# Keys two blocks ahead in a merged attention stage, magnitude pieces on VectorE, and semaphores cleared one stage later

## The chip, the cores and the metric

The kernel runs on one core of one Trainium2 chip. The metric is the device time of one execution in microseconds; lower is better. The time before is the median of three runs.

## The reference

A gated two-layer block on 2048 tokens of width 512 (x and a context of the same size). Layer 0 is a cross attention with 16 heads of 128 and a routed expert FFN; layer 1 is an attention in which the 16 heads of one token attend to each other, and an FFN with weights rounded to -1, 0 and 1. The part that this case is about:

```python
x = x + jnp.tanh(g_ffn[0]) * _L0_ffn_ref(_layernorm(x), ...)          # top 2 of 8 experts + shared
x = x + jnp.tanh(g_xattn[1]) * _L1_xattn_ref(_layernorm(x), ctx, ctx, ...)
x = x + jnp.tanh(g_ffn[1]) * _L1_ffn_ref(_layernorm(x), w1, b1, w2, b2)

def _L1_xattn_ref(q, k, v, Wq, bq, Wk, bk, Wv, bv, Wo, bo):
    Q = (q @ Wq.T + bq).reshape(bs, sl, H, HD)      # H = 16, HD = 32
    K = (k @ Wk.T + bk).reshape(bs, sl, H, HD)
    V = (v @ Wv.T + bv).reshape(bs, sl, H, HD)
    score = jnp.einsum('bshd,bsgd->bshg', Q, K)     # heads against heads, per token
    weight = jax.nn.softmax(score, axis=-1)
    attn = jnp.einsum('bshg,bsgd->bshd', weight, V).reshape(bs, sl, nf)
    return attn @ Wo.T + bo
# _bit_quant(w): scale = mean(|w|); ternary = clip(round(w / scale), -1, 1)
```

## The kernel before

The program is four stages, one after the other, each with its own streams for SyncE (all DMA issues of the stage but gathers), GpSimd, ScalarE, TensorE and VectorE: `l0_attention` (prefix a_), `l0_experts` (b_), `l1_attention` (p_, the merged stage) and `l1_output_ffn` (f_). The helper `stage` (L2607) runs one, ends it with a barrier of all engines, and then has GpSimd clear every semaphore of the stage, one instruction each, before GpSimd enters the next stage.

**The merged stage** does three things over four blocks of 512 tokens. It adds the experts' rows to x (two gathers by GpSimd, L1806, and `tile_stats` on VectorE, four 128-token tiles a block) and normalises each tile (`tile_normalise`). It projects keys, values and queries. And it does the attention of heads against heads. The operand splits (`w_high`, `c_high`, `h_high` on ScalarE, `..._low` on VectorE or GpSimd) give each fp32 operand a high and a low part, so a projection of one 128x512 piece is 12 matmuls.

The work of the first two kinds is a list `ITEMS`, in the order in which TensorE does it: ("k", b, j), ("v", b, j), ("q", b, j) are projections of piece j of block b, and ("h", b, j) is the transpose of the normalised tile j, which the queries need. Two PSUM banks take the items in turn, so item i waits until item i-2 was taken out. Each k, v or q piece goes through one of four slots of `outs` to DRAM (`store`), and a block's four pieces are then read back in the attention's layout (`load_k`, `load_v`, `load_q`). For the queries ScalarE then makes one more copy, `move_queries` (L1912). `ROUND` counts how often a slot has been used.

**The loop** goes over 32 pairs p, eight a block (b = p // 8, w = p % 8). Pair p does, on TensorE: `scores(p)` for two units, an item, `turn` of the two units of the pair before, a second item, and `weigh` for the pair before that. VectorE masks each unit's scores (L2150), finds the maxima (L2154), and takes the reciprocals (L2158); ScalarE does eight exponentials (L1924), takes k and q items (L1888) or the high part of h items (L1895), and copies the turned units out (L1930); GpSimd normalises (L1829). The first FIRST = 24 items run ahead of the loop, the other 40 two to a pair, so pairs 0 to 19 hold items and pairs 20 to 31 (`lean`) hold none. In a lean pair VectorE takes the reciprocal of the second unit after the mask and maxima of the next pair's first.

Beside the pairs from p = 12 on, 32 pieces of the FFN's weights are summed by magnitude for the last stage: one a pair on ScalarE, and from p = 20 one more on VectorE.

Instruction order on each engine is written out by hand. SyncE's order decides when a load or store is even tried: whatever stands behind a wait there waits too.

## Time and profile before

| | us |
|---|---|
| median of 3 runs (2204.09 to 2206.22) | 2206.16 |
| the profiled execution | 2200.77 |
| its span, first to last instruction | 2199.0 |
| merged stage: ScalarE's first instruction | 1481.47 |
| merged stage: first scores (pair 0) | 1581.19 |
| merged stage: scores of pairs 8, 16 | 1642.10, 1709.22 |
| merged stage: turns after the last pair | 1831.76 |
| last stage: first matmul of the output projection | 1849.20 |

TensorE is busy for 1969.6 us of the span (90%), GpSimd 1094.9, VectorE 1017.7, ScalarE 826.7. Times in the rows are microseconds from the span's start. A row of the timeline has the start, the time from the first start to the last end, engine, line, operation and tiles, and in brackets how long the engine stood idle ahead of it and who ended that.

### The profile page before, as it was taken

To read this page: it belongs to the slowest core of one execution; us is meant where nothing else is said; L and a number is where in the kernel's file an instruction comes from. 1 tells how busy PE (TensorE), PEld (TensorE's weight loads), DVE (VectorE), ACT (ScalarE), POOL (GpSimd) and SP (SyncE) were. 2 spreads that over 40 slices of the span, in tenths; PEclk is the share of its full clock that TensorE was granted. 3 is DMA by queue.
4 is the path that set the end of the run, shared out by engine and by line. 5 is a ranking of instruction groups with operands and counts; after the bars stand their busy time and mean duration, and the time that the engine had idled before them with its cause. 6 is when DMAs were issued, how large, how long until landed. Compare 5 with 4: busy or idle time off the path is not lost. (4 is left out here: it accounts for less than half of the span.)

```text
span 2199.0 us, 30241 instructions
## 1 busy us (share of the span) xinstructions
PE 1969.6 (90%) x10428; PEld 1649.3 (75%) x10428; DVE 1017.7 (46%) x1561; ACT 826.7 (38%) x1578; POOL 1094.9 (50%) x805
## 2 busy tenths in 40 slices
PE   6999999999999999689996999985799874789998
PEld 5888788878887888478884899983677653568886
DVE  3556654755476547623331333335466343583111
ACT  3336332633363336231211222223377763233332
POOL 6755576557655774441147646606254222533332
PEclk9999999999999999879998999997899966899999
DMA  4232323133313331362326655427676635222000
GB/s 155 82 105 68 116 96 106 53 108 116 107 48 112 101 124 30 118 214 82 139 95 204 197 164 161 131 75 210 175 187 153 169 113 184 81 68 67 19 19 19
DMA packets 173869, 251.29 MB, mean 114 GB/s; under 512 B 45040, under 2 KB 69616, under 8 KB 173744
## 3 DMA queue, kind: packets, MB, share of 16 engines
q1 hardware_dynamic: 158656, 205.23, 30.0%
q0 software_dynamic: 9472, 34.09, 4.9%
q10 hardware_dynamic: 5616, 10.23, 1.2%
q8 instruction: 88, 1.44, 0.3%
q14 instruction: 37, 0.30, 0.0%
HBM read 182.92 MB, written 66.58 MB: 113 GB/s over the span
## 5 line engine op out<-in xcount | busy, mean ns | idle before, releaser
L238 POOL TENSOR_TENSOR a_w_hl<-a_w_raw,a_w_hl 128x2048 fp32r<-128x2048 f32 x65 | 299.8, 4613 | 164.6 <-ACT a_w_hl L300 164.4
L413 PE MATMUL a_proj<-a_c_hl,a_w_hl 128*128 128x512 f32 x768 | 183.2, 399 | 21.4 <-DVE a_w_hl L530 19.6
L300 ACT ACTIVATE a_w_hl<-a_w_raw 128x2048 fp32r<-128x2048 f32 x66 | 126.2, 1912 | 164.6 <-PE a_proj L413 106.7
L413 PEld LDWEIGHTS a_proj<-a_c_hl,a_w_hl 128*128 128x128 f32 x768 | 146.2, 192 | 53.8 <-issue 19.6
L487 PE MATMUL a_proj<-a_w_hl,a_a_hl 128*128 128x512 f32 x768 | 179.5, 392 | 4.0 <-DVE a_a_hl L586 4.0
L413 PE MATMUL a_proj<-a_w_hl,a_c_hl 128*128 128x512 f32 x768 | 181.3, 392 | 0.0
L413 PE MATMUL a_proj<-a_a_hl,a_w_hl 128*128 128x512 f32 x768 | 176.4, 390 | 0.0
L319 ACT ACTIVATE a_sq<-a_proj,a_vecs 128x512 f32<-128x512 f32 x128 | 87.9, 689 | 228.6 <-PE a_proj L413 149.1
L487 PEld LDWEIGHTS a_proj<-a_w_hl,a_a_hl 128*128 128x128 f32 x768 | 142.7, 188 | 34.3 <-POOL a_w_hl L238 5.5
L413 PEld LDWEIGHTS a_proj<-a_a_hl,a_w_hl 128*128 128x128 f32 x768 | 143.6, 188 | 29.7
L262 POOL TENSOR_TENSOR a_ssum<-a_ssum,a_sq 128x512 f32<-128x512 f32 x112 | 145.6, 1300 | 36.9 <-ACT a_sq L319 33.2
L413 PEld LDWEIGHTS a_proj<-a_w_hl,a_c_hl 128*128 128x128 f32 x768 | 142.4, 188 | 28.7
L1252 PE MATMUL b_gate_up<-b_wts,b_xt_hl 128*128 x936 | 159.4, 326 | 4.2 <-DVE b_xt_hl L1451 4.2
L1252 PEld LDWEIGHTS b_gate_up<-b_wts,b_xt_hl 128*128 128x128 f32 x936 | 154.5, 190 | 8.2 <-issue 5.0
L2398 POOL TENSOR_TENSOR f_a_hl<-f_act_sb,f_a_hl 128x512 fp32r<-128x512 f32 x64 | 86.0, 1345 | 149.0 <-ACT f_a_hl L2430 148.9
L1160 PE MATMUL b_gate_up<-b_wts 128*128 128x512 f32 (+1 forms) x576 | 142.0, 407 | 3.0 <-POOL b_wts L937 2.5
L586 DVE SCALAR_TENSOR_TENSOR a_a_hl<-a_qT,a_vecs,a_a_hl 128x512 fp32r<-128x512 f32 x64 | 105.1, 1672 | 83.4 <-ACT a_a_hl L333 83.4
L1160 PEld LDWEIGHTS b_gate_up<-b_wts 128*128 128x128 f32 (+1 forms) x576 | 106.8, 186 | 34.3 <-POOL b_wts L937 2.6
L2490 PE MATMUL f_totals<-f_ternary,f_a_hl 128*128 128x512 f32 x512 | 122.5, 396 | 0.0
L2476 PE MATMUL f_hidden<-f_h_hl,f_ternary 128*128 x512 | 121.0, 394 | 0.0
L1829 POOL TENSOR_TENSOR p_probs<-p_probs,p_rden 128x512 f32<-128x512 f32 x64 | 68.0, 1068 | 99.6 <-DVE p_rden L2158 99.1
L1924 ACT ACTIVATE p_probs<-p_probs,p_mx 128x128 f32<-128x128 f32 x256 | 99.1, 390 | 47.5 <-DVE p_mx L2154 47.4
(245 smaller groups left out, 3682.5 us busy)
## 6 DMA issues: line engine op xcount, KB each, us to landing
a_w_raw<-in_a_ki_w SPq DMA_DIRECT2D x18, 1024.0 KB, 5.2
a_w_raw<-in_a_vi_w SPq DMA_DIRECT2D x16, 1024.0 KB, 5.1
a_w_raw<-in_a_q_w SPq DMA_DIRECT2D x16, 1024.0 KB, 5.1
a_w_raw<-in_a_o_w SPq DMA_DIRECT2D x16, 1024.0 KB, 5.4
b_gu_raw<-in_b_gate_up POOLq DMA_DIRECT2D x32, 352.0 KB, 3.7
l_sorted_rows<-b_zeros SPq DMA_DIRECT2D x39, 256.0 KB, 3.3
b_hs<-l_sorted_rows SPq DMA_DIRECT2D x39, 256.0 KB, 3.2
l_expert_out<-b_yg ACTq DMA_DIRECT2D x39, 256.0 KB, 3.5
```

The source lines that it names most:

```text
L238: pool.tensor_tensor(w_hl[:, s, 1], w_raw[:, s], f32(w_hl[:, s, 0]), ALU.subtract)\
L262: pool.tensor_tensor(ssum[:], first, sq[:, n % 2, :], ALU.add).then_inc(sq_added, 1)
L300: act.activation(w_hl[:, i % 2, 0], w_raw[:, i % 2], ACT.Copy).then_inc(w_high, 1)
L319: act.activation(sq[:, n % 2, :], proj[:, j, :], ACT.Square, bias=bias)\
L413: mm = pe.matmul(proj[:, j, :], left, right, start=(k == 0 and n == 0), stop=(k == KC - 1 and n == 2))
L487: mm = pe.matmul(proj[:, j, :], a_hl[:, ap, k, j * P:(j + 1) * P], w_hl[:, i % 2, wp, k], start=(n == 0 and m == 0), stop=(n == 4 * G - 1 ...
L586: dve.scalar_tensor_tensor(a_hl[:, 1, n % 4, :], qT[:, n, :], v_b[:, n:n + 1], f32(a_hl[:, 0, n % 4, :]), ALU.add, ALU.subtract).then_inc( ...
L1160: mm = pe.matmul(gu_ps[0:w, n, part, :], gu_hl[:, s, wp, k, cols], h_hl[:, hslot, ap, k, :], start=(k == 0 and m == 0), stop=(k == KC - 1 ...
L1252: mm = pe.matmul(gu_ps[:, i % 2, half, 0:F], x_part(i, xp)[:, own], part(r, P, at, F), start=(k == 0 and xp == 0 and start == HI), stop=(k ...
L1924: e = act.activation(probs[:, r, y, :], probs[:, r, y, :], ACT.Exp, bias=mx[:, r, y:y + 1], accum_out=den[:, r, y:y + 1])
L2476: mm = pe.matmul(h_ps[:, m % 2, :], w_t[:, 2 * g, k, f * P:(f + 1) * P], h_hl[:, ap, k, bass.ds(BLK * t, BLK)], start=(k == 0 and ap == 0) ...
L2490: mm = pe.matmul(y_ps[:, j, :], a_hl[:, ap, f, j * P:(j + 1) * P], w_t[:, 2 * g + 1, f, :], start=(m == 0 and ap == 0), stop=(m == NG * FC ...
```

## The change

Three things change, all in the merged stage but for the last.

1. `ITEMS` is ordered anew. Ahead of the loop stand k0, v0, h0, q0 and k1 (20 items; before k0, v0, h0, q0, h1, q1). In the loop each block b has v(b+1), h(b+1), q(b+1) and k(b+2), in this order, so the keys are two blocks ahead. Pairs 0 to 21 hold items, 22 to 31 are lean. All that serves the items moves with them: the tiles' stats from w = 0..3 to w = 4..7, the context's splits from w = 4..7 to w = 2..5, `move_queries` from w = 3 to w = 7, and SyncE's stores and loads. Ahead of the loop the low parts of the query weights go from GpSimd to VectorE, between the tiles' stats; the stats of block 1 come after all four h items of block 0; GpSimd splits one piece of context after each gather.
2. The magnitude pieces: pairs 16 to 21 one on VectorE, pairs 22 to 27 two on VectorE and one on ScalarE, pairs 28 to 31 two on VectorE (before 20 on ScalarE and 12 on VectorE, now 6 and 26).
3. The semaphores of a stage are cleared by GpSimd at the end of its stream for the next stage, ahead of that stage's barrier; those of the last stage after its barrier, as before.

In the diff stand, one after the other: the list, the pieces, GpSimd ahead of the loop and in it, ScalarE the same, VectorE ahead of the loop, and `stage`.

```diff
-    ITEMS = [(kind, b, j) for kind, b in (("k", 0), ("v", 0), ("h", 0), ("q", 0), ("h", 1), ("q", 1)) for j in range(4)]
+    ITEMS = four("k", 0) + four("v", 0) + four("h", 0) + four("q", 0) + four("k", 1)
     FIRST = len(ITEMS)
     for n in range(1, NBLK):
-        ITEMS += [("k", n, j) for j in range(4)]
+        ITEMS += four("v", n) + four("h", n) + four("q", n)
         if n + 1 < NBLK:
-            ITEMS += [("v", n, 0), ("h", n + 1, 0), ("v", n, 1), ("h", n + 1, 1), ("h", n + 1, 2), ("h", n + 1, 3),
-                      ("v", n, 2), ("v", n, 3)]
-            ITEMS += [("q", n + 1, j) for j in range(4)]
-        else:
-            ITEMS += [("v", n, j) for j in range(4)]
+            ITEMS += four("k", n + 1)
...
-        for p in range(12, NP * NBLK):
-            PIECES += [(p, "act")] + ([(p, "dve")] if p >= 20 else [])
+        for p in range(16, NP * NBLK):
+            PIECES += [(p, "dve")] * (1 if p < 22 else 2) + [(p, "act")] * (22 <= p < 28)
...
             for n in range(TPB):
                 power(n)
                 gather(n + 2)
-            for k in range(KC):
-                w_low("q", k)
             for n in range(TPB, 2 * TPB):
                 power(n)
                 gather(n + 2)
-                if n == TPB + 1:
-                    for k in range(KC):
-                        c_low(1, k)
+                c_low(1, n - TPB)
...
-                if b + 2 < NBLK and w >= NP - KC:
-                    c_low(b + 2, w - NP + KC)
+                if b + 2 < NBLK and 2 <= w < 2 + KC:
+                    c_low(b + 2, w - 2)
...
-            for j in range(TPB):
-                h_high_part(1, j)
             for j in range(4):
-                take("q", 1, j)
-                if j == 2:
+                take("k", 1, j)
+                if j == 1:
                     move_queries(0)
...
-                    if b + 1 < NBLK and w == 3:
+                    if b + 1 < NBLK and w == 7:
                         move_queries(b + 1)
...
             for j in range(TPB):
-                tile_stats(TPB + j)
                 h_low_part(0, j)
-                tile_normalise(TPB + j)
-            for j in range(TPB):
-                h_low_part(1, j)
+            tile_stats(TPB)
+            for n in range(TPB + 1, 2 * TPB):
+                tile_stats(n)
+                tile_normalise(n - 1)
+            tile_normalise(2 * TPB - 1)
...
         run(nc, new_sem, *args)
+        for s in used:
+            nc.gpsimd.sem_clear(s)
         nc.all_engine_barrier()
-        for s in own:
-            nc.gpsimd.sem_clear(s)
+        used[:] = own
```

**SyncE at the head of the merged stage.** The names: l_kT, l_vT are the stored keys and values, p_k the keys' read back (`load_k`), carry<-in_ctxT the context's load, x<-p_xr the store of x2, p_xr<-x_shared the load of x. Before:

```order
L1682 DMA l_kT<-p_outs 128x512 x4
L1661 DMA carry<-in_ctxT 128x512 x4
L1671 DMA x<-p_xr 128x512 x4
L1703 DMA p_k<-l_kT 32x16x128 x4
L1680 DMA l_vT<-p_outs 128x16x32
L1667 DMA p_xr<-x_shared 128x512
```

and now:

```order
L1681 DMA l_kT<-p_outs 128x512
L1660 DMA carry<-in_ctxT 128x512
L1702 DMA p_k<-l_kT 32x16x128 x4
L1670 DMA x<-p_xr 128x512 x4
L1679 DMA l_vT<-p_outs 128x16x32
L1666 DMA p_xr<-x_shared 128x512
```

(the first two are the last of four such turns: keys and context alternate). The keys' read moved ahead of the four x2 stores, and each context load stands right behind a key store.

**TensorE in the loop.** p_scores are a pair's scores, p_turned its turns, p_out its weighing; p_proj is an item (from p_w_hl,p_c_hl values, from p_ident,p_hn an h item). Pair 2 before:

```order
L2043 MATMUL p_scores<-p_k,carry 128x128 x8
L2028 MATMUL p_proj<-p_w_hl,p_c_hl 128x512 x12
L2052 MATMUL p_turned<-p_ident,p_probs 128x128 x8
L2008 MATMUL p_proj<-p_ident,p_hn 128x128 x4
L2065 MATMUL p_out<-p_probs,p_v 32x128 x8
```

and now:

```order
L2033 MATMUL p_scores<-p_k,carry 128x128 x8
L1998 MATMUL p_proj<-p_ident,p_hn 128x128 x4
L2042 MATMUL p_turned<-p_ident,p_probs 128x128 x8
L1998 MATMUL p_proj<-p_ident,p_hn 128x128 x4
L2055 MATMUL p_out<-p_probs,p_v 32x128 x8
```

Before, pairs 2 and 3 each held a value and an h item, and pair 4 two h items; now pairs 2 and 3 hold two h items each, and the queries come right behind them.

**GpSimd at the start of the merged stage.** ISA x84 are the clears of the experts' semaphores, x58 those of the first stage's. Before:

```order
L2618 ISA x84
L1799 UNCONDITIONAL_BRANCH
L1832 MEMSET p_ones 128x128
L1833 MEMSET p_mhalf 128x1
L1834 IOTA p_diff 128x8
```

and now:

```order
L2612 ISA x58
L1795 UNCONDITIONAL_BRANCH
L1828 MEMSET p_ones 128x128
L1829 MEMSET p_mhalf 128x1
L1830 IOTA p_diff 128x8
```

The 58 stand ahead of the barrier that ends the experts' stage, the 84 were behind it; they now stand behind the merged stage's last normalisation.

## Rows read from the trace of the kernel before

**Rows 1.** The windows view of the head: PE, PEld, DVE, ACT, POOL busy, clock, DMA.

```profile
1520.00:1530.00 10.00, 0.00 (x0) 0.00 (x0) 1.74 (x3) 0.00 (x0) 4.46 (x4) 0.56 1.01 209
```

**Rows 2.** Timeline from the end of the first stage to the start of the second.

```profile
921.76 1.77 SPq L858 DMA_DIRECT2D carry<-x  x4
...
925.83 0.20 POOL L913 MEMSET b_ones<- 128x128 f32 x1 [7.47 <-issue]
...
926.79 0.69 DVE L1296 BATCH_NORM_STATS2 b_stats<-carry 128x6 f32<-128x512 f32 x1 [7.89 <-POOL b_tile_no L918]
```

**Rows 3.** Timeline at the start of the merged stage.

```profile
1481.47 0.63 ACT L1876 ACTIVATE p_w_hl<-carry 128x512 fp32r<-128x512 f32 x1 [7.20 <-PEq L2616]
...
1487.16 0.20 POOL L1832 MEMSET p_ones<- 128x128 f32 x1 [60.93 <-issue]
...
1490.04 4.48 PE L2028 MATMUL p_proj<-p_c_hl,p_w_hl 128*128 128x512 f32 x9 [12.13 <-DVE p_c_hl L2094]
```

**Rows 4.** Timeline at the start of the last stage.

```profile
1847.91 2.91 DVE L2519 TENSOR_TENSOR f_a_hl<-f_act_sb,f_a_hl 128x512 fp32r<-128x512 f32 x2 [5.28 <-ACT f_a_hl L2414]
```

**Rows 5.** Timeline of the merged stage's head, ahead of its first scores.

```profile
1508.91 0.75 DVE L2102 SCALAR_TENSOR_TENSOR p_xr<-p_routed,weight,p_xr 128x512 f32<-128x512 f32 x1 [1.40 <-DMA p_routed<-l_expert_out,place]
...
1519.69 5.93 SPq L1667 DMA_DIRECT2D p_xr<-x_shared  x1
...
1528.19 0.75 DVE L2102 SCALAR_TENSOR_TENSOR p_xr<-p_routed,weight,p_xr 128x512 f32<-128x512 f32 x1 [9.85 <-DMA p_xr<-x_shared]
...
1531.69 0.99 POOL L1806 DMA_INDIRECT p_routed<-l_expert_out,place  x1 [0.18 <-issue]
...
1538.22 6.82 POOL L1812 TENSOR_TENSOR p_c_hl<-carry,p_c_hl 128x512 fp32r<-128x512 f32 x4 [0.43 <-ACT p_c_hl L1872]
...
1539.18 1.09 DVE L2102 SCALAR_TENSOR_TENSOR p_xr<-p_routed,weight,p_xr 128x512 f32<-128x512 f32 x1 [3.18 <-DMA p_routed<-l_expert_out,place]
...
1549.53 10.78 PE L2028 MATMUL p_proj<-p_a_hl,p_w_hl 128*128 128x512 f32 x34 [13.03 <-DVE p_a_hl L2126]
```

**Rows 6.** Timeline of TensorE in the loop over the 32 pairs.

```profile
1581.19 1.16 PE L2043 MATMUL p_scores<-p_k,carry 32*128 32x128 f32 x16
...
1582.29 5.76 PE L2028 MATMUL p_proj<-p_c_hl,p_w_hl 128*128 128x512 f32 x24
...
1595.62 1.16 PE L2043 MATMUL p_scores<-p_k,carry 32*128 32x128 f32 x16
...
1642.10 1.16 PE L2043 MATMUL p_scores<-p_k,carry 32*128 32x128 f32 x16
...
1739.12 1.16 PE L2043 MATMUL p_scores<-p_k,carry 32*128 32x128 f32 x16
...
1747.82 1.16 PE L2043 MATMUL p_scores<-p_k,carry 32*128 32x128 f32 x16
...
1815.20 1.11 PE L2052 MATMUL p_turned<-p_ident,p_probs 128*128 128x128 f32 x4 [2.13 <-POOL p_probs L1829]
...
1822.04 1.11 PE L2052 MATMUL p_turned<-p_ident,p_probs 128*128 128x128 f32 x4 [2.14 <-POOL p_probs L1829]
...
1831.76 1.14 PE L2052 MATMUL p_turned<-p_ident,p_probs 128*128 128x128 f32 x8
```

**Rows 7.** Groups by line, 1400 to 2199: busy us, mean ns, idle before.

```profile
L1924 ACT ACTIVATE p_probs<-p_probs,p_mx 128x128 f32<-128x128 f32 x256 | 99.1, 390 | 47.5 <-DVE p_mx L2154 47.4
...
L1930 ACT ACTIVATE p_probs<-p_turned 128x512 f32<-128x512 f32 x64 | 34.1, 584 | 0.0
...
L1895 ACT ACTIVATE p_a_hl<-p_proj 128x512 fp32r<-128x512 f32 x16 | 9.4, 589 | 30.2 <-PE p_proj L2008 30.2
...
L1912 ACT ACTIVATE carry<-carry 128x2048 f32<-128x2048 f32 x4 | 7.6, 1904 | 0.0
...
L2150 DVE TENSOR_TENSOR p_probs<-p_scores,p_mask 128x512 f32<-128x512 f32 x64 | 43.6, 681 | 68.8 <-PE p_scores L2043 68.7
...
L2154 DVE TENSOR_REDUCE p_mx<-p_probs 128x4 f32<-128x512 f32 x64 | 43.9, 686 | 2.2
```

More of the change, by code:

```diff
@@ L1685, in landed @@
                 for j in range(4):
-                    sp.wait_ge(stored[j], 16 * (ROUND[kind, b] + 1))
+                    sp.wait_ge(stored[j], 16 * (ROUND[kind, b, j] + 1))
             def load_q(b):
@@ L1741, in _ @@
                 store_x2(1, j)
-            for j in range(TPB):
-                load_x(2, j)
-            for j in range(2):
-                store("q", 1, j)
+            store("k", 1, 0)
+            store("k", 1, 1)
             for p in range(NP * NBLK):
@@ L1748, in _ @@
                 n = b + 1
-                if n < NBLK:
-                    if w == 0:
+                if w == 0:
+                    if b and n < NBLK:
+                        store_x2(n, TPB - 1)
+                    if n < NBLK:
+                        store("k", n, 2)
+                        store("k", n, 3)
+                    if b + 2 < NBLK:
+                        for k in range(KC):
+                            load_ctx(b + 2, k)
+                if n < NBLK:
+                    if w == 1:
+                        store("v", n, 0)
+                        store("v", n, 1)
+                        load_k(n)
+                    elif w == 2:
+                        store("v", n, 2)
+                        store("v", n, 3)
+                    elif w == 3:
+                        load_v(n)
+                    elif w == 5:
+                        store("q", n, 0)
+                        store("q", n, 1)
+                    elif w == 6:
@@ L1751, in _ @@
                         store("q", n, 2)
                         store("q", n, 3)
[L1753 removed]
                         load_q(n)
[L1755 to L1772 removed]
+                if b + 2 < NBLK:
+                    if w == 2:
+                        for j in range(TPB):
+                            load_x(b + 2, j)
+                    if 5 <= w:
+                        store_x2(b + 2, w - 5)
+                    if w == 7:
+                        store("k", b + 2, 0)
+                        store("k", b + 2, 1)
@@ L1849, in _ @@
                 gather(n + 2)
-                if n == TPB + 1:
-                    for k in range(KC):
-                        c_low(1, k)
+                c_low(1, n - TPB)
             for p in range(NP * NBLK):
                 b, w = p // NP, p % NP
-                n = TPB * (b + 2) + w
-                tile = b + 2 < NBLK and w < TPB
+                n = TPB * (b + 2) + w - 4
+                tile = b + 2 < NBLK and w >= 4
                 if tile:
@@ L1955, in _ @@
                 take("q", 0, j)
-            for j in range(TPB):
-                h_high_part(1, j)
             for j in range(4):
-                take("q", 1, j)
-                if j == 2:
+                take("k", 1, j)
+                if j == 1:
                     move_queries(0)
@@ L2176, in _ @@
             tile_stats(0)
+            w_low("q", 0)
             tile_stats(1)
+            w_low("q", 1)
             tile_normalise(0)
+            tile_stats(2)
+            w_low("q", 2)
+            tile_normalise(1)
             dve.wait_ge(const_in, 32)
             take_v(0, 0)
-            tile_stats(2)
-            tile_normalise(1)
             take_v(0, 1)
             tile_stats(3)
+            w_low("q", 3)
             tile_normalise(2)
+            tile_normalise(3)
             take_v(0, 2)
-            tile_normalise(3)
             take_v(0, 3)
             for j in range(TPB):
-                tile_stats(TPB + j)
                 h_low_part(0, j)
-                tile_normalise(TPB + j)
-            for j in range(TPB):
-                h_low_part(1, j)
+            tile_stats(TPB)
[3 more added lines that the diff above has]
+            tile_normalise(2 * TPB - 1)
             for p in range(NP * NBLK):
                 b, w = p // NP, p % NP
-                n = TPB * (b + 2) + w
-                tile = b + 2 < NBLK and w < TPB
+                n = TPB * (b + 2) + w - 4
+                tile = b + 2 < NBLK and w >= 4
                 mask_scores(2 * p)
@@ L2631, in build @@
             stage(l1_output_ffn, x2, aT, part("d_"), a["w_ffn"], sums, out)
+    for s in used:
+        nc.gpsimd.sem_clear(s)
     last[0].close()
```

49 lines of the change are left out of this document (11 added, 38 removed).

## The prediction

> **What bounds the kernel now.** The windows view shows where the chip does nothing. In the merged stage's head there are 10 us in which TensorE and ScalarE do no work at all while the DMA engines are busy throughout [rows 1]. So I went to the timeline of that stage. Its first scores, with which the loop begins, start at 1581.2, 99.7 us after ScalarE's first instruction at 1481.5 [rows 3, 6], and of those TensorE needs 16 items of 2.9 us (24 matmuls in 5.76 [rows 6]), 46 us, and a few us for eight transposes. The rest is waits: for the second block's x tile (VectorE idle 9.85 us until 1528.2), for a gather (3.18), for four context splits on GpSimd (6.82 us in one piece, with the next tile's power queued behind), and at the end TensorE idle for 13.03 us until 1549.5 [rows 5]. From the first scores on TensorE's order sets the time: a pair with two projected items takes 8.70 us (1747.82 - 1739.12), and the twelve lean pairs 83.9 (1831.76 - 1747.82), 7.0 each [rows 6]. In a lean pair no engine is full; a ring of work is: mask, maxima and reciprocal on VectorE, normalisation, turn, weigh, scores, and TensorE waits 2.14 us in it for GpSimd [rows 6]. The third place is the start of a stage, where GpSimd first clears semaphores: it is 4.07 us behind SyncE at the second stage [rows 2] and 5.69 behind ScalarE at the merged stage [rows 3].
>
> **The clears (part 3).** At the second stage VectorE's first statistics wait 7.89 us for GpSimd's constants [rows 2]. With the clears gone these are ready at 922.7; then x is late, issued at 921.76. How long it takes to land no row here shows; the gain is 4.1 us less what the load needs past 922.7, so between 0 and 4.1, and I take the middle and a little, 2.3, since the load is as small as any. TensorE is fed by VectorE there and moves with it. At the merged stage TensorE's first matmul waits 12.13 us for VectorE, which waits for GpSimd [rows 3]; ScalarE's first two high parts are ready 1.6 us after its start, so the start moves from 1490.0 to 1484.3, 5.7 us, counted in the head below. At the last stage VectorE's wait ends with ScalarE, behind a load, not with GpSimd [rows 4]: nothing. Where the clears go they cost: 84 of them, 5.8 us at the rate of rows 3, behind the merged stage's last normalisation, where the last turns (1831.8 [rows 6]) and the last stage's first split (1847.9 [rows 4]) are 16 us apart, filled by the last weighing and the stores of the heads; 58 behind the experts' GpSimd work, which is over 60.9 us before the stage is [rows 3]. Nothing, with 0 to 1 us as bound.
>
> **The head.** I follow the new order. Keys 0 take four items, 11.6 us, and some 2 while their splits come one by one, to 1498; two value items until 1504. The third needs the first taken out, and VectorE takes it only after the statistics of tile 2, which wait for a gather until 1508.9 before [rows 5], 1503.2 now, then with one more weight split and a normalisation until 1507.6. Values end at 1513.4, the four h items go back and forth over two banks (a transpose, a high part of 0.59, a low part of 0.69, as for any 512 columns [rows 7]) until 1518.1, and the queries follow at once, since the h items no longer share VectorE with block 1's statistics. Before, they began at 1549.5 [rows 5]. Queries end at 1530. Then the keys of block 1 need four context splits on GpSimd, one behind each gather of tiles 4 to 7. Statistics of tile 4 from 1518.1, 2.5 us each (two additions of 0.75, one pass of 0.69, two small ones); power and the two gather instructions 3.2 (0.99 each and what lies between); split 1.7 (6.82 / 4); a gather lands 7.5 us after its issue (1531.69 to 1539.18) [rows 5]. So: tile 4 done 1520.6, its gather for tile 6 issued 1521.4, landed 1528.8, tile 6 done 1531.3; tile 7 waits for tile 5's gather until 1533.8, done 1536.3, its gather until 1539.6, fourth split 1541.2. TensorE idles 11 us, so it starts at the low clock: 34 matmuls took 10.78 us after such an idle time [rows 5] against 8.2 at full rate, 2.6 us lost. Keys 1 end at 1541.2 + 11.6 + 2.6 = 1555.4, in round numbers 1555.2, and scores start there instead of at 1581.2: **26.0 us less**. x of block 1 must be there at 1518; store and load are issued 7.6 us earlier than before, with the keys' read long ahead of them. Bounds of this term: the split could be 4 us earlier, or x as late behind its store as before.
>
> **The loop.** Same 32 pairs, but four more items in it (44). The order has three consequences.
> (a) Two pairs of h items on end. In such a pair TensorE has little to do (8.70 less two items of 2.9, and 1.4 for two transposes: 4.3 us), so ScalarE and VectorE set the pace: VectorE may not mask pair 3 before it has taken both low parts of pair 2, which wait for ScalarE behind eight exponentials (3.1 us) and two copies (1.0) [rows 7]. From pair 2's scores at 0: masks and maxima to 3.9, exponentials 2.6 to 5.7, low parts at 7.0 and 8.5, masks of pair 3 to 11.2, exponentials 9.9 to 13.0, low parts at 14.3 and 15.8. The queries need all four: TensorE stands from 12.5 to 15.8, and pair 5 starts at 23.4 and ends at 32.1 (0.5 more where heads are copied). So pairs 2 to 5 take 32.1 to 32.6.
> (b) `move_queries` (1.90 [rows 7]) now stands at the end of w = 7 and the next scores wait for it: ScalarE is through at 10.95 after that pair's scores, not 8.70, so 2.25 a block.
> (c) The waits of the keys for the context's splits go; a pair of keys or values takes 8.70.
> Block 0: 14.4 for pairs 0 and 1 as before (1595.62 - 1581.19 [rows 6]), 32.1, 17.4, 2.25: 66.2, against 60.9 (1642.10 - 1581.19). Block 1: 17.4 + 32.6 + 17.4 + 2.25 = 69.7. Then pairs 16 to 21: 50.0, and ten lean pairs: 83.9 less two of 6.84 (the ring's period: 1822.04 - 1815.20 [rows 6]) = 70.2. SyncE's read of block 3's queries stands in pair 22 ahead of the pieces' loads, so ScalarE waits for a piece and then moves the queries: 3.7, bounds 0 and 6. In all 66.2 + 69.7 + 50.0 + 70.2 + 3.7 = 259.8, before 250.6 (1831.76 - 1581.19 [rows 6]): **9.2 us more**. Bounds: 0, if (a) and (b) are hidden, to 14.
>
> **The pieces (part 2).** A lean pair's time is the ring's, in which ScalarE isn't: it already idles for VectorE (47.4 us over the stage [rows 7]). So one piece less on it brings nothing, and two on VectorE, 0.69 us each as any such reduction [rows 7], end before the next mask. 0, bounds -1 and +3 (three loads a pair through two buffers).
>
> **Sum:** -2.3 - 26.0 + 9.2 = **-19.1 us**. On the profiled execution 2200.8 - 19.1 = 2181.7; its own time is 5.4 below the median of the three runs, so I forecast 2206.2 - 19.1 = 2187.1.
>
> **Rivals.**
> Full pace (0.23): (a) and (b) cost nothing, the head as forecast. The loop then stays at 250.6: -28.3, 2177.9. For it: TensorE ran the first block in 60.9 with h items in it. Against: the in-order chain in (a).
> Late x (0.15): block 1's x tile lands as late behind the values' store as before, 10 us, or later, for SyncE stood 5.93 us in that load's issue [rows 5], and the read of the block's statistics shifts by some 9 us. -19.1 + 9 = -10.1, 2196.1. The values' store goes out in runs of 32 floats. The Trainium skill, page "DMA: Bandwidth & Descriptors", Specifications, gives 512 bytes as the least transfer for full rate and says that below it the engine reads and writes back; by that rule the store, unchanged in size, stays slow and this rival gains weight; rows 5 agree in that the load behind it was held up.
> Clears absorbed (0.05): the loads, not GpSimd, set both stage starts: -19.1 + 8.0 = -11.1, 2195.1.
> Slower (0.03): `move_queries` at w = 7 waits for its read. I reckon the read landed 8 us ahead of need (stored after pair 5, read in pair 6). If it comes 14.4 us later than that, each of three blocks loses 6.4 and the 19.1 are gone; at 17 us late each loses 9, in all +7.9, 2214.1.
> The forecast's own case has 0.54, with 2181 to 2193.
>
> **How the numbers follow.** The range leaves out the slower case and the far ends: 2176 to 2198. A measurement of this kernel can tell about 0.2%, 4.4 us. Faster by more: all cases but the last and a little of the two weak ones, 0.93; same 0.04; slower 0.03.
>
> **What would show it.** In the profile after: first matmul of the merged stage some 5.7 us closer to ScalarE's first instruction; queries' items 31 us earlier, ended by VectorE's low part; TensorE idle about 11 us for GpSimd's context split ahead of the keys of block 1; first scores 74 us after the stage's start, not 100; TensorE waiting about 3 us for the low parts ahead of each block's queries; scores of pairs 8, 16 and 24 behind `move_queries`; lean pairs at 6.8 us as before. I am wrong if the head shrinks by less than 15 us, or if pairs 2 to 5 take 29 us.

## The result: 2221.8 us, slower than before

The changed kernel took 2221.78 us (median of 5 runs, 2217.3 to 2224.5), the kernel before 2204.09 (5 runs beside it). The ratio is 1.0082, with a 95% interval from 1.0060 to 1.0103: 13 to 23 us slower, where I had forecast 19 us faster and left slower a chance of 0.03. The profiled execution took 2222.94 us, its span is 2221.1; of before the span is 2199.0.

The two profiled spans, cut at TensorE's rows (us, each worked out from the starts and lengths of its rows in the timeline):

| stretch | before | after | difference |
|---|---|---|---|
| up to the end of the experts' last matmul | 1477.91 | 1484.22 | +6.31 |
| to the merged stage's first matmul | 12.13 | 10.10 | -2.03 |
| to the first scores (the head) | 91.15 | 75.76 | -15.39 |
| pairs 0 to 7 | 60.91 | 71.26 | +10.35 |
| pairs 8 to 15 | 67.12 | 76.81 | +9.69 |
| pairs 16 to 21 | 51.79 | 54.91 | +3.12 |
| pairs 22 to the last weighing | 73.96 | 75.14 | +1.18 |
| to the end of the span | 364.03 | 372.90 | +8.87 |

The first line is mostly spread: over the twelve profiles of this study the experts' last matmul ends anywhere from 1475.8 to 1484.7 us, and of those with the clears as they were before from 1477.2 to 1481.7. The other lines repeat within 2 us between profiles of kernels that agree in the stretch. They add up to +15.8, which is inside the interval. So two things I had priced at nothing or at little took the time: the last stage's way in and out (+8.9), and the loop (+24.3 where I had said +9.2). One run of the kernel before, of the 35 beside four of the experiments below, took 6831 us and is left out of their ratios.

**The start of the merged stage after.** Timeline; the columns are start, length, engine, line, operation, out<-in, and in brackets the idle time before it and what ended it.

```profile
1479.80 4.42 PE L1272 MATMUL b_y_sum<-b_wts,b_a_hl 128*128 x18
...
1484.25 0.69 DVE L1462 COPY b_yg<-b_y_sum 128x512 f32<-128x512 f32 x1 [1.39 <-PE b_y_sum L1272]
...
1491.40 0.20 POOL L1828 MEMSET p_ones<- 128x128 f32 x1 [58.85 <-POOLq L2613]
...
1491.42 0.63 ACT L1868 ACTIVATE p_w_hl<-carry 128x512 fp32r<-128x512 f32 x1 [10.85 <-PEq L2613]
...
1494.32 1.19 PE L2018 MATMUL p_proj<-p_c_hl,p_w_hl 128*128 128x512 f32 x2 [10.11 <-DVE p_c_hl L2084]
```

GpSimd and ScalarE now start together, and TensorE follows 2.9 us behind them, not 8.6 as in [rows 3]: that is the 5.7 us I had expected. But ScalarE's idle time ahead of the stage has grown from 7.20 us [rows 3] to 10.85. All engines stand 3.65 us longer, and GpSimd's own bracket shows why this was not hidden: it had been idle for 58.85 us when the stage began, with 58 clears to do in that time. The trace has each clear with its time: the 58 run from 1487.38 to 1491.09 us, and the last engine to reach the end of the experts' stage, SyncE, did so at 1487.19.

The clears stand behind the end of the stage's Block (the part of the program that holds the five streams), and this end itself gathers all engines. GpSimd clears only when the last engine has arrived, and the barrier written behind the clears lets nobody go before them. Before, the same clears stood behind both, so that only GpSimd was late. At the last stage it is 84 clears, from 1855.28 to 1860.94:

```profile
1848.25 0.60 ACT L1931 ACTIVATE p_o<-p_out 128x512 f32<-128x512 f32 x1 [1.17 <-PE p_out L2055]
...
1861.31 0.19 DVE L2498 TENSOR_REDUCE f_sum<-magnitudes 128x2 f32<-128x32 f32 x1 [16.77 <-PEq L2613]
...
1868.15 1.22 PE L2444 MATMUL f_totals<-f_a_hl,f_h_hl 128*128 128x512 f32 x2 [5.63 <-DVE f_a_hl L2514]
```

**The head after.** TensorE, then the two additions of tile 6 on VectorE, then the fourth context split on GpSimd:

```profile
1530.37 12.74 PE L2018 MATMUL p_proj<-p_a_hl,p_w_hl 128*128 128x512 f32 x48 [1.50 <-DVE p_a_hl L2116]
1556.25 13.90 PE L2018 MATMUL p_proj<-p_c_hl,p_w_hl 128*128 128x512 f32 x48 [13.14 <-POOL p_c_hl L1808]
1570.08 1.16 PE L2033 MATMUL p_scores<-p_k,carry 32*128 32x128 f32 x16
```

```profile
1540.46 0.75 DVE L2092 SCALAR_TENSOR_TENSOR p_xr<-p_routed,weight,p_xr 128x512 f32<-128x512 f32 x1 [4.21 <-DMA p_routed<-l_expert_out,place]
1541.24 2.29 DVE L2095 SCALAR_TENSOR_TENSOR p_xr<-p_routed,weight,p_xr 128x512 f32<-128x512 f32 x1
```

```profile
1554.59 1.51 POOL L1808 TENSOR_TENSOR p_c_hl<-carry,p_c_hl 128x512 fp32r<-128x512 f32 x1
```

The queries start 39.0 us into the stage (I said 36.6), the keys of block 1 at 64.8 (59.7), the scores at 78.7 (73.7): the head is shorter by what the new order promised, less 5 us. The 13.14 us ahead of the keys end with GpSimd's last split.

**The loop after.** Pairs 4 and 5, the first key item of block 0, and the step to pair 8; then, from the windows view, the stretch of pair 4 (its last three numbers are the granted clock, the DMA share and GB/s):

```profile
1596.92 1.16 PE L2033 MATMUL p_scores<-p_k,carry 32*128 32x128 f32 x16
1600.31 5.46 PE L2018 MATMUL p_proj<-p_a_hl,p_w_hl 128*128 128x512 f32 x12 [2.23 <-DVE p_a_hl L2116]
...
1606.79 2.98 PE L2018 MATMUL p_proj<-p_a_hl,p_w_hl 128*128 128x512 f32 x12
...
1610.70 1.16 PE L2033 MATMUL p_scores<-p_k,carry 32*128 32x128 f32 x16
...
1621.96 3.01 PE L2018 MATMUL p_proj<-p_c_hl,p_w_hl 128*128 128x512 f32 x12 [1.39 <-POOL p_c_hl L1808]
...
1641.34 2.08 PE L2033 MATMUL p_scores<-p_k,carry 32*128 32x128 f32 x16 [3.06 <-issue]
1643.35 4.91 PE L2018 MATMUL p_proj<-p_w_hl,p_c_hl 128*128 128x512 f32 x12
```

```profile
1596.90:1610.70 13.80, 11.57 (x66) 9.22 (x64) 7.95 (x16) 9.79 (x31) 6.29 (x6) 0.75 0.05 20
```

The waits are where I had placed them: for the low parts ahead of the queries (2.23), and for the move of the queries ahead of pair 8 (3.06). What I had not counted stands in the same rows. The item behind the wait takes 5.46 us, not 2.98, and the scores of pair 8 take 2.08, not 1.16, with 4.91 for the item behind them: these matmuls run at TensorE's lower level (1.2 GHz) in place of the upper (2.4) for all or most of their time. The first stop so costs 2.5 us beyond its own length, the second 2.9. In the trace of after the same happens again at 1677.8 (4.58 us behind 2.25 of waiting), at 1754.0 (5.46 behind 2.82), and the item behind pair 16's scores takes 4.52 after 2.05 of waiting: 1.5 to 2.5 us more each.

### The profile page after: what moved, and what is told of

Same layout as the page of the kernel before. It is cut to its first block and busy times, and to the rows that moved or that the text cites. A ratio compares the mean times of both kernels' runs of the same rounds, so it can differ in the third digit from the quotient of the medians.

```text
span 2221.1 us, 30227 instructions
## 1 busy us (share of the span) xinstructions
PE 1985.5 (89%) x10428; PEld 1663.1 (75%) x10428; DVE 1029.7 (46%) x1579; ACT 819.8 (37%) x1550; POOL 1091.0 (49%) x801
## 5 line engine op out<-in xcount | busy, mean ns | idle before, releaser
L1916 ACT ACTIVATE p_probs<-p_probs,p_mx 128x128 f32<-128x128 f32 x256 | 99.1, 388 | 74.1 <-DVE p_mx L2144 74.1
```

What stands on the lines that cost most here:

```text
L1916: e = act.activation(probs[:, r, y, :], probs[:, r, y, :], ACT.Exp, bias=mx[:, r, y:y + 1], accum_out=den[:, r, y:y + 1])
```

## The experiments

The theory after the result, called A in the expectations: the clears join everybody's path, and four places stop TensorE, three in the loop (two transposes h on end; the context's split; the late move of the queries) and one in the head (GpSimd's order), each costing more than its own length through the clock. Ratios are to the kernel before, run beside each, with their 95% intervals; 12 runs of each kernel and 23 to 35 of before, 5 of the last kernel.

| kernel | median us | ratio | interval |
|---|---|---|---|
| clears_only | 2212.52 | 1.0038 | 1.0024 to 1.0052 |
| before_inside | 2198.64 | 0.9978 | 0.9962 to 0.9994 |
| order_only | 2210.66 | 1.0032 | 1.0015 to 1.0048 |
| pieces_only | 2198.39 | 0.9978 | 0.9962 to 0.9994 |
| mixed | 2208.18 | 1.0018 | 1.0004 to 1.0032 |
| hv | 2201.42 | 0.9994 | 0.9978 to 1.0009 |
| fill | 2214.03 | 1.0041 | 1.0026 to 1.0056 |
| move6 | 2206.54 | 1.0011 | 0.9995 to 1.0028 |
| c_first | 2210.03 | 1.0024 | 1.0008 to 1.0041 |
| all | 2172.07 | 0.9853 | 0.9830 to 0.9876 |

And the stretches of their profiled spans, as above ("in": from the experts' last matmul to the stage's first; "22 on": to the last weighing; "out": to the end of the span):

| kernel | in | head | 0 to 7 | 8 to 15 | 16 to 21 | 22 on | out |
|---|---|---|---|---|---|---|---|
| before | 12.13 | 91.15 | 60.91 | 67.12 | 51.79 | 73.96 | 364.0 |
| clears_only | 10.11 | 90.24 | 61.13 | 66.21 | 51.26 | 74.58 | 372.7 |
| before_inside | 6.45 | 91.20 | 60.91 | 66.81 | 51.67 | 74.07 | 364.3 |
| order_only | 12.12 | 75.03 | 70.21 | 77.14 | 53.60 | 77.07 | 364.4 |
| pieces_only | 12.12 | 90.64 | 61.77 | 65.44 | 47.87 | 72.50 | 364.8 |
| after | 10.10 | 75.76 | 71.26 | 76.81 | 54.91 | 75.14 | 372.9 |
| mixed | 10.12 | 75.91 | 66.92 | 72.28 | 51.33 | 76.91 | 372.3 |
| hv | 10.10 | 73.44 | 64.24 | 71.45 | 49.25 | 78.54 | 372.8 |
| fill | 10.11 | 76.02 | 69.26 | 72.72 | 53.95 | 75.28 | 372.9 |
| move6 | 10.11 | 73.82 | 66.86 | 71.55 | 53.15 | 71.47 | 372.9 |
| c_first | 10.11 | 65.99 | 72.83 | 73.70 | 53.66 | 77.38 | 372.8 |
| all | 6.47 | 61.30 | 62.28 | 68.80 | 48.84 | 74.86 | 364.7 |

### The clears: clears_only and before_inside

clears_only is the kernel before with the new `stage` and nothing else. before_inside clears the same semaphores at the same stage, but at the end of GpSimd's stream inside the Block, in each of the four stages:

```
+def clear_used(pool):
+    for s in USED:
+        pool.sem_clear(s)
 ...
         @block.gpsimd
         def _(pool):
             ...
+            clear_used(pool)
 ...
         run(nc, new_sem, *args)
-        for s in used:
-            nc.gpsimd.sem_clear(s)
         nc.all_engine_barrier()
-        used[:] = own
+        USED[:] = own
```

> The kernel before with the moved clears alone. Theory A (the clears join the path: the end of a Block gathers all engines first, GpSimd clears only then, and the all-engine barrier behind it holds everybody): 3.6 us more ahead of the merged stage (58 clears), 5.5 more ahead of the last (84 clears), 3.2 more at the very end (63 clears), less the 5.7 by which the merged stage's first matmul comes earlier in its stage, so 4 to 7 us slower than before. Theory B (my prediction's: the clears are hidden, only the gains count): 6 to 8 us faster. In the trace, theory A wants the merged stage's first instruction about 7.2 us behind the last matmul of the second stage, as against 3.6 in the kernel before.

> The kernel before with each stage's semaphores cleared in the next stage, at the end of GpSimd's own stream inside the Block, so ahead of the gathering of the engines. Theory A (what costs is only that the clears stand behind the gathering): the clears are hidden beside the last weighing of each stage, the merged stage's first matmul still comes 5.7 us earlier, so 5 to 8 us faster than before. Rival (the clears cost their time wherever they stand, or the early start of GpSimd brings nothing): within 2 us of before, or slower.

clears_only is 8.1 us slower by the medians, 8.4 by the ratio, just above the 4 to 7 expected; before_inside is 5.8 faster by the medians, 4.9 by the ratio. ScalarE's first instruction of the merged stage comes 7.2 us behind the experts' last matmul in clears_only, 3.6 in the kernel before, as expected. ScalarE's first instruction of the merged stage and VectorE's first of the last stage, in clears_only:

```profile
1483.00 0.63 ACT L1876 ACTIVATE p_w_hl<-carry 128x512 fp32r<-128x512 f32 x1 [10.85 <-PEq L2618]
...
1842.45 0.19 DVE L2503 TENSOR_REDUCE f_sum<-magnitudes 128x2 f32<-128x32 f32 x1 [17.04 <-PEq L2618]
```

and in before_inside, with TensorE's first matmul between them:

```profile
1482.88 0.63 ACT L1879 ACTIVATE p_w_hl<-carry 128x512 fp32r<-128x512 f32 x1 [7.20 <-PEq L2629]
...
1485.78 1.62 PE L2031 MATMUL p_proj<-p_c_hl,p_w_hl 128*128 128x512 f32 x3 [6.45 <-DVE p_c_hl L2097]
...
1837.93 0.19 DVE L2507 TENSOR_REDUCE f_sum<-magnitudes 128x2 f32<-128x32 f32 x1 [11.40 <-PEq L2629]
```

58 clears hold everybody for 10.85 - 7.20 = 3.65 us and 84 for 17.04 - 11.40 = 5.64: 63 and 67 ns each. At the very end 63 more stand in everybody's path: from the last instruction that works to the end of the span it is 10.0 us in clears_only and 6.0 before, 63 ns each. Inside the Block they cost nothing that a row shows, and the merged stage starts 5.7 us earlier after the experts' last matmul (6.45 for 12.13). The last column says the same of the way out: 364.3 against 372.7. The idea was sound; three lines further up it would have been a gain, where it was put it is a loss.

### The order without the clears: order_only

```
         run(nc, new_sem, *args)
-        for s in used:
-            nc.gpsimd.sem_clear(s)
         nc.all_engine_barrier()
-        used[:] = own
+        for s in own:
+            nc.gpsimd.sem_clear(s)
```

> The changed kernel with the old clearing (own semaphores, behind the barrier): the new order of items, tiles, stores and pieces alone. Theory A (the loop's new stalls each pull TensorE's clock down with them): from the two profiled spans the head gives 15 us back (21.05 less the 5.66 that come from the clears) and the loop takes 24.6, so 7 to 12 us slower than before. Rival (the order is fine, the loss is mostly the clears and the spread of the runs): 0 to 10 us faster than before.

6.2 us slower by the medians, 7.1 by the ratio; the head gives 16.1 back and the loop takes 24.2. With the 8.1 of clears_only that makes 14.3 of the 17.7 by which the changed kernel is slower; the 3 between lie inside the intervals. The head and the loop keep their size whatever is done with the clears, so what the order costs and what the clears cost can be told apart.

### The pieces alone: pieces_only

```
-        for p in range(12, NP * NBLK):
-            PIECES += [(p, "act")] + ([(p, "dve")] if p >= 20 else [])
+        for p in range(16, NP * NBLK):
+            PIECES += [(p, "dve")] * (1 if p < 22 else 2) + [(p, "act")] * (22 <= p < 28)
```

> The kernel before with the new distribution of the magnitude pieces alone (from pair 16 on VectorE, one and from pair 22 two a pair, six on ScalarE in pairs 22 to 27). The prediction gave it 0, from -1 to +3 us, since the lean pairs are set by the turn of the probabilities and neither engine is full there: within 2 us of before, the lean pairs still 6.8 us. Rival (a second piece a pair on VectorE delays the reciprocals that GpSimd waits for): ten lean pairs by 0.5 us and more, 5 us or more slower.

Both theories missed it: 4.9 us faster. The gain is not in the lean pairs (73.96 to 72.50) as much as in pairs 8 to 21 (118.9 to 113.3), where I had not looked. In the kernel before ScalarE's pieces stood among the context's splits, and the key item that waits for the last split stopped TensorE long enough for the clock to fall. Pair 16 before (the split's high part and the pair's own piece on ScalarE, then TensorE), and in pieces_only:

```profile
1709.83 1.19 ACT L1872 ACTIVATE p_c_hl<-carry 128x512 fp32r<-128x512 f32 x1
1710.85 0.69 ACT L1917 ACTIVATE p_w_piece<-p_w_piece 128x512 f32<-128x512 f32 x1
...
1712.75 4.43 PE L2028 MATMUL p_proj<-p_c_hl,p_w_hl 128*128 128x512 f32 x12 [2.37 <-POOL p_c_hl L1812]
```

```profile
1711.40 1.12 ACT L1872 ACTIVATE p_c_hl<-carry 128x512 fp32r<-128x512 f32 x1
...
1714.26 3.01 PE L2028 MATMUL p_proj<-p_c_hl,p_w_hl 128*128 128x512 f32 x12 [1.39 <-POOL p_c_hl L1812]
```

2.37 us of waiting with 4.43 behind it became 1.39 with 3.01: pair 16 is 2.4 us shorter. The piece at 1710.85 starts behind the high part and cannot be what held it; the one in front is that of pair 15, 0.66 us at 1704.05. Without it the high part starts 0.30 us ahead of pair 16's scores (1711.70), not 0.61 behind them (1709.22). So 2.4 us come from an instruction of 0.7. Pair 12 is shorter by the same 2.4 us (8.54 to 6.14), and the rest of the 5.6 between pairs 8 and 21 I have not traced. If the gain is as large in the new order, for order_only holds these pieces too, the order of the items by itself costs about 6.2 + 4.9 = 11 us.

### Two transposes on end: mixed and hv

```
 mixed
-        ITEMS += four("v", n) + four("h", n) + four("q", n)
+        ITEMS += [("v", n, 0), ("h", n, 0), ("v", n, 1), ("h", n, 1), ("h", n, 2), ("h", n, 3), ("v", n, 2), ("v", n, 3)]
+        ITEMS += four("q", n)
 hv
+        ITEMS += [(kind, n, j) for j in range(4) for kind in ("h", "v")] + four("q", n)
 both, on ScalarE and on GpSimd (c_low)
-                    if b + 2 < NBLK and 2 <= w < 2 + KC:
-                        c_high_part(b + 2, w - 2)
+                    if b + 2 < NBLK and w in (3, 4):
+                        c_high_part(b + 2, 2 * w - 6)
+                        c_high_part(b + 2, 2 * w - 5)
```

> The changed kernel with one thing altered in the loop: the transposes h stand among the values v again (v0, h0, v1, h1, h2, h3, v2, v3), and the context's split stands two pieces a pair behind them. Theory A (the loss in the loop is the wait for the low parts of h, 2.2 to 2.8 us a block, and the item behind it at half the clock, 5.5 us for 3.0, and the same in small at the first key item): 3 blocks by about 5 us and 2 by about 2.5, so 14 to 20 us faster than the changed kernel, 2202 to 2208 us. Rival (VectorE's and ScalarE's chain of scores sets the pace of a pair, so that TensorE's stalls hide elsewhere): less than 4 us faster than the changed kernel, 2217 or more.

> The changed kernel with its loop order altered in one respect: each pair that had two transposes h now has one h and one v (h0 v0 h1 v1 h2 v2 h3 v3), the stores of the values follow, and the context's split stands in pairs 3 and 4, two pieces each. The move of the queries stays late, the head and the clears stay. Theory A (two transposes in one pair make TensorE stand for VectorE's low parts, 2.2 to 2.7 us, and the item behind runs at half the clock; with the order v0 h0 v1 h1 h2 h3 v2 v3, which kept one such pair a block, 13.6 us of it went): no 5.5 us item is left behind an h, and the loop is another 3 blocks by 4 to 5 us shorter, so 2194 to 2198. Rival (what is left is set by VectorE and ScalarE): no better than that mixed order, 2205 or more.

In both, the stores of the values follow their items. mixed gives back 13.6 us, just under the 14 to 20 expected, and hv 20.4; 24 to 28 had been expected, and it has half of the further step. Both runs alter two things, the place of the transposes and that of the context's split, so their gain belongs to both: the waits of the key items for the split (1.39 and 1.41 us in the changed kernel, 4.57 for the item behind the second) are 0.7 at most in mixed and gone in hv. mixed keeps one pair of two transposes a block, and behind it TensorE still stops and slows:

```profile
1584.45 5.49 PE L2020 MATMUL p_proj<-p_w_hl,p_c_hl 128*128 128x512 f32 x12 [2.67 <-DVE p_a_hl L2118]
```

The kernel before has such a pair of transposes too, in the same order among the values, and there the wait is 1.27 us and the clock stays up:

```profile
1616.81 3.02 PE L2028 MATMUL p_proj<-p_w_hl,p_c_hl 128*128 128x512 f32 x12 [1.27 <-DVE p_a_hl L2126]
```

So it is not the pair of transposes alone that makes the stop. What else does, the tiles' stats and the splits at other places beside it or its own place two pairs earlier in the block, no run here separates. In hv the item at that place takes 3.02 us without a wait:

```profile
1589.17 3.02 PE L2017 MATMUL p_proj<-p_w_hl,p_c_hl 128*128 128x512 f32 x12
```

Pairs 0 to 21 are 18.0 us shorter than in the changed kernel, the lean ones 3.4 longer. The loss is at pair 24, where TensorE still waits for the late move, and the ring then runs several pairs at the lower clock:

```profile
1767.91 2.08 PE L2032 MATMUL p_scores<-p_k,carry 32*128 32x128 f32 x16 [5.97 <-issue]
...
1775.59 2.08 PE L2032 MATMUL p_scores<-p_k,carry 32*128 32x128 f32 x16
```

7.68 us from the one to the next, not 6.84 [rows 6].

### The clock by itself: fill

The wait stays; TensorE is only kept busy in it.

```
                     if kind == "q":
+                        for m in range(8 if b else 0):
+                            pe.matmul(proj[:, i % 2, :], w_hl[:, 0, 0, m % KC, 0:P], w_hl[:, 0, 0, m % KC, :],
+                                      start=True, stop=True)
                         pe.wait_ge(h_split, TPB * b + TPB)
```

> The changed kernel, and in blocks 1 to 3 TensorE does eight throwaway matmuls of 128x512 (a weight tile by itself, into the bank that the next item overwrites) ahead of its wait for the last low part of h, that is in the 2.2 to 2.8 us in which it stood there. Nothing else is altered, the wait stays. Theory A (the stall costs twice, because the item behind it runs at half the clock): the q item behind the wait takes about 3.0 us instead of 4.6 to 5.5, so 2 us a block and 5 to 7 us in all faster than the changed kernel, about 2215. Rival (the clock there falls for another reason, or the slower item is hidden beside VectorE's and ScalarE's chain): within 2 us of the changed kernel's 2221.8.

7.8 us faster than the changed kernel by the medians (9.0 by the ratios), a little over the 5 to 7 expected. The throwaway matmuls and the item behind the wait:

```profile
1590.60 2.12 PE L2007 MATMUL p_proj<-p_w_hl 128*128 128x512 f32 x8 [0.72 <-DVE p_a_hl L2119]
1592.55 2.89 PE L2021 MATMUL p_proj<-p_a_hl,p_w_hl 128*128 128x512 f32 x12
```

2.89 us, where the changed kernel has 5.46 at this place. No engine has less to do than in the changed kernel, and one has more; only the clock differs. This is the run that shows that a stop is paid a second time behind it.

### The late move of the queries: move6

```
-                    if b + 1 < NBLK and w == 7:
+                    if b + 1 < NBLK and w == 6:
                         move_queries(b + 1)
```

> The changed kernel with the move of the next block's queries one pair earlier on ScalarE (behind pair 6 of the block, where ScalarE idles 3.5 us for the next maxima, not behind pair 7, where TensorE stands for it). Theory A (TensorE waits 2 to 5.6 us at each block's first scores for this move, and the scores and the item behind run at half the clock): 3 to 4 us at each of the two blocks with items behind, 5 us at the last, 10 to 13 us faster than the changed kernel, about 2210. Rival (the read of the queries has not landed a pair earlier, so ScalarE stands and its exponents with it): the same or slower than 2221.8.

15.2 us faster than the changed kernel, more than the 10 to 13 expected. The loop is 15.1 us shorter by the stretches. The read had landed in time but for 1.20 us of ScalarE's, and pair 8 starts with no wait and at full clock:

```profile
1625.57 1.92 ACT L1904 ACTIVATE carry<-carry 128x2048 f32<-128x2048 f32 x1 [1.20 <-DMA carry<-l_qT]
...
1632.77 1.16 PE L2033 MATMUL p_scores<-p_k,carry 32*128 32x128 f32 x16
1633.86 3.06 PE L2018 MATMUL p_proj<-p_w_hl,p_c_hl 128*128 128x512 f32 x12
```

### GpSimd's order in the head: c_first

```
+            for k in range(KC):
+                c_low(1, k)
             for n in range(TPB, 2 * TPB):
                 power(n)
                 gather(n + 2)
-                c_low(1, n - TPB)
```

> The changed kernel with GpSimd splitting the four context pieces of block 1 in the head ahead of the powers and gathers of block 1's tiles, not one behind each gather. Theory A (the keys of block 1, and with them the first scores, wait for nothing but GpSimd's order): the last piece is there at about 47 us of the stage instead of 64, TensorE goes from the queries to the keys without a stop and at full clock, and the first scores come 12 to 15 us earlier, so 2207 to 2211. Rival (the first scores wait for the move of the queries anyway): the keys come early, the scores 4 us or less earlier, 2217 or more.

```profile
1530.97 7.81 POOL L1808 TENSOR_TENSOR p_c_hl<-carry,p_c_hl 128x512 fp32r<-128x512 f32 x4 [5.77 <-ACT p_c_hl L1865]
```

```profile
1543.34 11.04 PE L2019 MATMUL p_proj<-p_c_hl,p_w_hl 128*128 128x512 f32 x48
1560.79 1.62 PE L2034 MATMUL p_scores<-p_k,carry 32*128 32x128 f32 x11 [6.40 <-ACT carry L1905]
```

```profile
1558.73 1.91 ACT L1905 ACTIVATE carry<-carry 128x2048 f32<-128x2048 f32 x1 [8.49 <-DMA carry<-l_qT]
```

11.8 us faster than the changed kernel, inside the 2207 to 2211 expected, though the first scores come 9.8 us earlier, not 12 to 15. The keys follow the queries without a stop, 13 us earlier; 6.4 of that is given back to a new wait, the read of the queries. Both theories had a part in it.

### All of it: all

The clears inside the Block, c_first, hv and move6 together.

> The changed kernel with all that the theories name: the clears inside the Block at the end of GpSimd's own stream, the context of block 1 split ahead of the gathers, the order h0 v0 h1 v1 h2 v2 h3 v3 in the loop with the context's split behind it (pairs 3 and 4, two pieces each), the move of the queries a pair earlier. Theory A (the new order was sound, and lost by four places where an engine stands): clears 12, head 12, loop 18 us faster than the changed kernel with the stalls gone together, about 2175 to 2182, 22 to 30 us faster than before. Rival (VectorE's and ScalarE's work in the pairs with items is the bound once the stalls go): a pair with items stays above 8.7 us, and the whole at 2190 or more.

2172.07 us: 32 us faster than before by the ratio (1.7% at the most, 1.2% at the least), 49.7 faster than the changed kernel. The expectation had been 2175 to 2182. The four alone add up to more (some 12 of clears, 11.8, 20.4 and 15.2: 59). The overlap is in pairs 0 to 21: hv alone takes 18.0 us off them and move6 11.4, this kernel with both 23.1. The loop now takes 254.8 us, against 253.8 in the kernel before with its shorter list of items. ScalarE's idle time for the maxima, by line, in the changed kernel and in this one (busy us, mean ns, idle before it):

```profile
L1916 ACT ACTIVATE p_probs<-p_probs,p_mx 128x128 f32<-128x128 f32 x256 | 99.1, 388 | 74.1 <-DVE p_mx L2144 74.1
```

```profile
L1918 ACT ACTIVATE p_probs<-p_probs,p_mx 128x128 f32<-128x128 f32 x256 | 99.0, 390 | 40.8 <-DVE p_mx L2147 40.8
```

It went from 47.4 [rows 7] up to 74.1 and down to 40.8. The longest stop left in the head is the wait for the moved queries ahead of the first scores:

```profile
1548.36 2.08 PE L2036 MATMUL p_scores<-p_k,carry 32*128 32x128 f32 x16 [3.65 <-ACT carry L1906]
```

## Why the prediction was wrong, step by step

In the prediction's terms the sum was -2.3 - 26.0 + 9.2 = -19.1 us. With what the traces show in their place it is -1.6 - 21.1 + 24.3, and 12.5 for the clears that had been put at nothing: +14.1, beside +17.7 by the medians.

**The clears.** The gains were read rightly. At the merged stage it was 5.7, as said, and at the last stage nothing (364.3 us for the way out in before_inside, 364.0 before). At the second stage VectorE's first statistics stood 5.0 us behind SyncE's first load [rows 2]; now it is 3.45 us, with the wait ended by that load:

```profile
924.32 2.30 SPq L858 DMA_DIRECT2D carry<-x  x4
...
927.77 0.69 DVE L1296 BATCH_NORM_STATS2 b_stats<-carry 128x6 f32<-128x512 f32 x1 [6.31 <-DMA carry<-x]
```

1.6 us (1.0 in clears_only), for 2.3 said. The step that failed is "Where the clears go they cost ... nothing, with 0 to 1 us as bound". I looked for idle time of GpSimd ahead of the stage, found 60.9 us of it, and took it as cover. But the clears could not use it: they stand behind the gathering at the Block's end, and I had not asked what releases the first of them. 3.65 us at the merged stage and 8.9 from its last weighing to the end, 12.5 us, with a bound of 1. (The rows of the last 8.9 are 5.64 at the last stage's start and 4.0 at its end; the last stage between them took 0.8 less.) The 12.5 us alone turn the forecast's -19.1 into -6.6.

**The head.** Direction and mechanism were right (queries released by VectorE's low part, keys of block 1 by GpSimd's split, TensorE idle 13 us where I had said 11), the size 5 us off: -15.4 and -5.7 at the start, 21 for the 26.0. The mis-sized term is the round from tile to gather to tile: from tile 4's first addition to the fourth split I had 23.1 us, and the trace has 25.6 (1530.47 to 1556.10). I took each addition at 0.75 us. The second additions of tiles 6 and 7 took 2.29 and 2.13, with no idle time ahead of them. It is not a gather that they stand for: the kernel waits for both gathers ahead of the first addition. They ran beside GpSimd's context splits:

```profile
1541.34 1.64 POOL L1808 TENSOR_TENSOR p_c_hl<-carry,p_c_hl 128x512 fp32r<-128x512 f32 x1
...
1548.02 1.53 POOL L1808 TENSOR_TENSOR p_c_hl<-carry,p_c_hl 128x512 fp32r<-128x512 f32 x1
```

Each addition starts within 0.1 us of such a split and ends 0.55 behind its end. In c_first, where no split stands beside tiles 6 and 7, the same two take 0.75, and those of tiles 4 and 5, which now have the splits beside them, 1.99 and 2.04. So the split behind each gather also slowed VectorE. That is not all of the round: in mixed and move6 these additions had no split beside them and took 0.75, and the head was still 75.9 and 73.8 us, since tile 6's first addition came 8.9 and 9.2 us behind the issue of its gathers, and 6.0 in the changed kernel. The rest of the 5 us is the 2.4 by which the queries start later. c_first shows that this whole round was the wrong thing to leave in the path: nothing but GpSimd's order put it there.

**The loop.** Said 9.2, measured 24.3. (a) The wait for the low parts is there, 2.2 to 2.8 us for the 3.3 said, but pairs 2 to 4 took 26.2 us for 23.4, since the first query item ran at half the clock. I had this cost in my hands, for I charged 2.6 us for it in the head, behind an idle time of 13; I did not ask whether stops of 2 to 3 us do the same. fill answers it. (b) The move of the queries cost 3.06 us of TensorE's time ahead of pair 8 and 2.9 through the clock, for 2.25 said; ahead of pair 24 the stop was 5.59; move6 brought 15.2 us in all. The rival "slower" had this place but another mechanism, a late read; the read was in time. (c) The keys' wait for the context's split did not go, it is 1.39 us for the 1.40 before, because the splits were spread over pairs 2 to 5, one each, up to the pair ahead of the keys. On the lean pairs I was right to 2 us.

**The pieces.** 0, from -1 to +3, said; -4.9 by the medians of pieces_only. I weighed them only where they are most, in the lean pairs, and not in pairs 12 to 21, where one of them lengthened a stop and with it held the clock down.

**The rivals.** Late x did not happen: the first addition of block 1 waited 0.25 us for its tile in the trace of after. So the rule of the Trainium skill that I had set beside it ("DMA: Bandwidth & Descriptors", Specifications, on transfers under 512 bytes) decided nothing here; SyncE still stood 4.33 us in the issue of the load behind the first store (5.93 in [rows 5]), but the load was early enough. Full pace failed for the same reason as the forecast. None of the rivals held the clears' cost.

**The tests I had set** (a head shorter by less than 15 us, pairs 2 to 5 in 29 us) would not have caught it: the head shrank by 15.4 and more, and the pairs were slow. They watched the terms I had doubts about and not the one that I had priced at nothing.

**Open.** Which stops pull the clock down is not settled. Key items behind 1.40 took 4.58 once and 3.02 once in the trace of fill, and in that of after 4.57 behind 1.41 and 3.01 behind 1.39. Behind 2.04 the scores of pair 8 in fill took 1.16 us and the item behind them 4.61; behind 2.05 in mixed they took 1.16 and 3.04. In the trace of after, no stop of 2.2 us or more ahead of an item was free of it, but in that of hv one of 2.37 was, with a granted clock of 1.00 behind it:

```profile
1701.47 1.16 PE L2032 MATMUL p_scores<-p_k,carry 32*128 32x128 f32 x16 [2.37 <-issue]
1702.56 0.66 PE L1997 MATMUL p_proj<-p_ident,p_hn 128*128 128x128 f32 x4
```

So the length of a stop alone does not decide. Open too is what lengthened the stop behind the transposes from 1.27 us before to 2.23 and more. And the last 3 us between the parts and the whole of the change are inside the spread.

## What to carry to other kernels

Idle time of an engine covers moved work only if the moved work can start in it: look at what releases its first instruction, and at whether a barrier that others pass stands behind it. The end of a Block was such a barrier here; what should be hidden goes inside. And when a stop of TensorE of some 2 us is priced, ask what the slower item behind it would add: here it was mostly 1.5 to 2.9 us on top of the wait, and eight matmuls nobody needs were cheaper than standing still. And look at what runs beside a short VectorE instruction on GpSimd before taking its time from another place.

## What the runs showed of the hardware

- Clearing a semaphore on GpSimd took 63 to 67 ns (58 in 3.65 us, 84 in 5.64), one after the other.
- A stop of TensorE of 2.23 us brought the granted clock from the upper to the lower level for the next item: 5.46 us for twelve 128x512 matmuls in place of 2.98; eight throwaway matmuls in the stop kept it up (2.89). Not every such stop did: behind one of 2.37 us in hv the clock stayed up.
- Without one 0.66 us instruction on ScalarE, ahead of what TensorE waited for, a pair was 2.4 us shorter, 0.98 of it the wait and 1.42 the clock.
- An addition of 128x512 on VectorE took 2.29 and 2.13 us in place of 0.75 while GpSimd split a context piece of 128x512 (1.64 and 1.53 us) beside it.
- The experts' last matmul ended anywhere from 1475.8 to 1484.7 us in six profiles of kernels that are alike up to there, so a difference of two profiled spans has to be cut at the stages before it is read.
